# A cross-attention and FFN kernel: work handed between engines is taken up a slot later, with four projection banks and one bank for p times V

## The reference

```python
h = _layernorm(x)                                # x: 32 batches x 64 rows x 512
q = (h @ Wq)                                     # 32 heads of 128, Wq 512 x 4096
k, v = ctx @ Wk, ctx @ Wv                        # 8 heads of 128 each
q, k = rope(q), rope(k)                          # tables gathered by position
scores = where(mask == 0, -1e9, q k^T / sqrt(128))   # four q heads share one k and v head
x = x + (softmax(scores) @ v) @ Wo
packed, scales = quantize_to_mxfp4(kernel)       # 512 x 512, blocks of 32 rows
x = x + _layernorm(x) @ dequantize(packed, scales) + bias
```

## Time and profile before

| what | value |
| --- | --- |
| median of 3 runs | 1244.49 us (1240.0 to 1246.65) |
| the profiled execution | 1243.1 us |
| its span, first to last instruction | 1240.9 us |
| PE busy | 1157.4 us, 93% |
| DVE busy | 1032.9 us, 83% |
| ACT busy | 653.5 us, 53% |
| POOL busy | 503.4 us, 41% |
| DMA | 67.41 MB, mean 54 GB/s |

### The profile page before, as it was taken

How to read it: one execution, slowest core, us unless ns; L and a number is a source line. 1 busy time by engine, 2 the same in 40 slices (tenths; PEclk the granted TensorE clock), 3 DMA queues, 4 the chain that set the end, 5 groups by cost and what they waited for, 6 DMA issues and landing times.

```text
span 1240.9 us, 19680 instructions
## 1 busy us (share of the span) xinstructions
PE 1157.4 (93%) x6308; PEld 983.0 (79%) x6320; DVE 1032.9 (83%) x2003; ACT 653.5 (53%) x2169; POOL 503.4 (41%) x394
## 2 busy tenths in 40 slices
PE   3799989999999999997988999999999999999987
PEld 2578878887888878886777788888888888888864
DVE  5878999899989999878888887787777877777786
ACT  3255545555555555645453545555555655555561
POOL 5353443335342443445543434433353434342322
PEclk7999999999999999998998999999999999999999
DMA  5220111112111021112312223111021112110003
GB/s 171 77 77 23 52 43 43 48 31 60 39 41 42 27 68 40 51 45 89 108 54 74 77 86 93 45 35 35 26 60 36 43 27 60 30 48 18 26 26 102
DMA packets 41476, 67.41 MB, mean 54 GB/s; under 512 B 8992, under 2 KB 11168, under 8 KB 41376
## 3 DMA queue, kind: packets, MB, share of 16 engines
q1 hardware_dynamic: 40608, 64.05, 17.6%
q0 software_dynamic: 768, 2.10, 0.5%
HBM read 61.94 MB, written 4.19 MB: 53 GB/s over the span
## 4 chain that ended last, share of the span: by engine, by line
PE 66%; DVE 19%; ACT 4%; issue 4%; DMA 4%; POOL 2%; SPq 0%; ACTq 0%; DVEq 0%; POOLq 0%
PE proj L379 11%; PE proj L380 11%; PE proj L381 10%; PE pO L379 6%; PE pS L468 6%; PE pO L380 6%; PE pO L381 6%; DVE t L728 2%; DVE t L729 2%; PE pV L495 2%; DMA raw<-wo 2%; PE pV L496 2%; PE pT L478 2%; ACT sm L641 2%; PE pO L512 1%
## 5 line engine op out<-in xcount | busy, mean ns | idle before, releaser
L952 POOL TENSOR_TENSOR qT<-qT,t 128x512 f32<-128x512 f32 x128 | 187.3, 1463 | 393.3 <-DVE t L729 393.2
L619 ACT ACTIVATE sm<-pS 128x256 f32<-128x256 f32 x128 | 49.3, 385 | 313.7 <-PE pS L468 313.5
L641 ACT ACTIVATE sm<-sm,tiny 128x64 f32<-128x64 f32 x512 | 172.0, 337 | 77.0 <-DVE tiny L847 75.2
L379 PE MATMUL proj<-XH,QH 128*128 128x512 f32 x512 | 204.8, 400 | 6.1 <-DVE VS L899 4.1
L380 PE MATMUL proj<-XL,QH 128*128 128x512 f32 x512 | 202.6, 396 | 0.0
L381 PE MATMUL proj<-XH,QL 128*128 128x512 f32 x512 | 202.6, 396 | 0.0
L379 PE MATMUL pO<-OH,AH 128*128 128x512 f32 x448 | 181.1, 404 | 12.1 <-DVE acc L815 12.0
L380 PE MATMUL pO<-OL,AH 128*128 128x512 f32 x448 | 176.6, 394 | 0.0
L381 PE MATMUL pO<-OH,AL 128*128 128x512 f32 x448 | 175.9, 393 | 0.0
L468 PEld LDWEIGHTS pS<-kT,qT 128*128 128x128 f32 x1024 | 134.7, 192 | 13.2 <-issue 3.1
L724 DVE TENSOR_TENSOR qT<-proj,COS 128x512 f32<-128x512 f32 x128 | 88.0, 687 | 68.0 <-PE proj L381 40.2
(11 more groups left out here) (129 smaller groups left out, 2565.2 us busy)
## 6 DMA issues: line engine op xcount, KB each, us to landing
raw<-wq SPq DMA_DIRECT2D x64, 256.0 KB
raw<-wo SPq DMA_DIRECT2D x64, 256.0 KB
acc<-x SPq DMA_DIRECT2D x16, 256.0 KB, 3.0
raw<-wk SPq DMA_DIRECT2D x16, 256.0 KB
raw<-ctxT SPq DMA_DIRECT2D x16, 256.0 KB
raw<-wv SPq DMA_DIRECT2D x16, 256.0 KB
rawm<-fbias SPq DMA_DIRECT2D x16, 256.0 KB, 2.8
out<-acc SPq DMA_DIRECT2D x16, 256.0 KB, 2.0
```

Of the source, the lines that this page charges most:

```text
L379: pe.matmul(dst, lh, rh, start=k == 0, stop=False)
L641: made = act.activation(v4[:, a], v4[:, a], ACT.Exp, bias=nmx[:, a:a + 1], accum_out=rsum[:, a:a + 1])
L952: pool.tensor_tensor(dst, dst, t2[:, :].rearrange("p (a t) -> p a t", t=64), ALU.add).then_inc(made, 1)
```

## The change

The order inside ACT's, DVE's and POOL's slots is new, `proj` has four banks instead of three, and the two halves of `pV` lie in one bank. No arithmetic instruction and no DMA is added or removed. PE's order stays, except that the transposes of the second half's rows come a slot earlier (`X_AT` starts at HALF - 5 instead of HALF - 4).

- ACT: the high parts of V, x, the FFN input and W4 are taken up in the slot after the one in which PE made them (n - 1), at the start of the slot, and `high(n, False)` follows them, ahead of the scores. AH moves behind the exponentials.
- DVE: V's low part, `x_low` and `f_low` are those of slot n - 1 and stand, with the streamed low parts and `quantise`, between the statistics and the rotation of q. The reciprocal and the product come before AL.
- POOL: `low(n, False)` comes before the rotation's addition.

```diff
-PROJ = 3
+PROJ = 4
-X_AT = {-2: 4, -1: 5, 0: 6, 1: 7} | {HALF - 4 + t: 8 + t for t in range(8)}
+X_AT = {-2: 4, -1: 5, 0: 6, 1: 7} | {HALF - 5 + t: 8 + t for t in range(8)}
-        pV = pb("pV", [128, 2, 512])
+        pV = pb("pV", [128, 2, 256])
@@ PE, scores
+                if m == 0:
+                    pe.wait_ge(a_cs, 16)
@@ ACT, slot n
                 high(n, True)
+                if v_tile(n - 1):
+                    v_high(n - 1)
+                for i, c in quant_parts(n - 1):
...
+                if n - 1 in X_AT:
+                    x_high(X_AT[n - 1])
+                if n - 1 in FFN_AT and not is_last(n - 1):
+                    f_high(FFN_AT[n - 1])
+                high(n, False)
                 if 0 <= m < PAIRS:
                     act.wait_ge(e_qk, m + 1)
...
-                if 0 <= m - 2 < PAIRS:
-                    act.wait_ge(e_pv, m - 1)
...
                     made.then_inc(a_ex, 1)
+                if 0 <= m - 2 < PAIRS:
+                    act.wait_ge(e_pv, m - 1)
...
@@ DVE, slot n
+                if v_tile(n - 1):
...
+                if n - 1 in X_AT:
+                    x_low(X_AT[n - 1])
+                if n - 1 in FFN_AT and not is_last(n - 1):
+                    f_low(FFN_AT[n - 1])
+                for i in streamed(n, False):
+                    if lo_on_dve(i):
...
+                for i, c in quant_parts(n):
+                    for step in PART[c] if c < 14 else ():
+                        quantise(i, step).then_inc(v_q, 1)
                 if 0 <= n < PAIRS:
                     s, h = n // 4, n % 4
                     dve.wait_ge(e_qp, n + 1)
...
-                if 0 <= m - 2 < PAIRS:
-                    dve.wait_ge(a_ah, m - 1)
...
                 if 0 <= m < PAIRS:
...
                     dve.tensor_tensor(v4, v4, rinv.unsqueeze(2).broadcast_to([128, 4, 64]), ALU.mult).then_inc(v_pn, 1)
+                if 0 <= m - 2 < PAIRS:
+                    dve.wait_ge(a_ah, m - 1)
...
@@ POOL, slot n
                 low(n, True)
+                low(n, False)
                 if 0 <= n < PAIRS:
                     add_turned(qT[:, n // 4 % 2, :, n % 4, :], v_qc, v_qs, n + 1, g_qr)
                 if n in FFN_AT and not is_last(n):
                     add_bias(FFN_AT[n])
-                low(n, False)
```

More of the change, by code:

```diff
@@ L257, in cs_turned @@
         def cs_turned(T):
-            where = (pS, pT, pO, pV[:, 0])[T] if T < 4 else pS
+            where = (pS, pT, pO, pV.rearrange("p b t -> p (b t)"))[T] if T < 4 else pS
             return where[:, 256:512].rearrange("p (k t) -> p k t", k=2)
@@ L604, in rope, with v_high @@
                 act.copy(SIN[:, c], cs_turned(T)[:, 1, :]).then_inc(a_cs, 1)
+            def v_high(n):
+                s, t = v_tile(n)
+                v = v_count(s, t)
+                b = BANK["v", v - 1]
+                act.wait_ge(e_vp, v)
+                if s >= 2:
+                    act.wait_ge(e_pv, 4 * (s - 2) + t + 1)
+                for i in range(2):
+                    act.copy(VS[ROWS[i], i, 4 * (s % 2) + t, :], proj[ROWS[i], b, 0:256]).then_inc(a_vh, 1)
             for T in range(4):
@@ L643, in _ @@
                     made.then_inc(a_ex, 1)
+                if 0 <= m - 2 < PAIRS:
+                    act.wait_ge(e_pv, m - 1)
+                    if m - 2 >= 2:
+                        act.wait_ge(e_op, m - 3)
+                    act.copy(AH[:, m % 2].rearrange("p h (b t) -> p b h t", b=2),
+                             pV[:, :, :].rearrange("p b (h t) -> p b h t", h=4)).then_inc(a_ah, 1)
                 if is_last(n):
                     f_high(FFN_AT[n])
-                high(n, False)
                 if n in ROPE_AT:
                     rope(ROPE_AT[n])
[L649 to L667, removed]
         @block.vector
@@ L819, in _ @@
                     statistics("f", FFN_AT[n])
+                if v_tile(n - 1):
+                    s, t = v_tile(n - 1)
+                    v = v_count(s, t)
+                    b = BANK["v", v - 1]
+                    dve.wait_ge(a_vh, 2 * v)
+                    for i in range(2):
+                        made = dve.tensor_tensor(VS[ROWS[1 - i], i, 4 * (s % 2) + t, :], proj[ROWS[i], b, 0:256],
+                                                 VS[ROWS[i], i, 4 * (s % 2) + t, :].bitcast(F32), ALU.subtract)
+                    made.then_inc(v_vl, 1)
+                if n - 1 in X_AT:
[4 more added lines that the diff above has]
+                    if lo_on_dve(i):
+                        _, kind, a, b = STREAM[i]
+                        hi, lo, _, view = weight(kind, a, b)
+                        dve.wait_ge(a_hi, i + 1)
+                        dve.tensor_tensor(lo, view(raw[:, i % RING, :]), hi.bitcast(F32),
+                                          ALU.subtract).then_inc(v_lo, 1)
+                for i, c in quant_parts(n):
+                    for step in PART[c] if c < 14 else ():
+                        quantise(i, step).then_inc(v_q, 1)
                 if 0 <= n < PAIRS:
@@ L869, in _ @@
                     dve.tensor_tensor(v4, v4, rinv.unsqueeze(2).broadcast_to([128, 4, 64]), ALU.mult).then_inc(v_pn, 1)
[L870 to L880, removed]
+                if 0 <= m - 2 < PAIRS:
+                    dve.wait_ge(a_ah, m - 1)
+                    dve.tensor_tensor(AL[:, m % 2].rearrange("p h (b t) -> p b h t", b=2),
+                                      pV[:, :, :].rearrange("p b (h t) -> p b h t", h=4),
+                                      AH[:, m % 2].rearrange("p h (b t) -> p b h t", b=2).bitcast(F32),
+                                      ALU.subtract).then_inc(v_al, 1)
                 k = mask_at(n)
@@ L892, in _ @@
                            (g_qr, n + 1))
[L893 to L910, removed]
         @block.gpsimd
```

21 lines of the change are left out of this document (11 added, 10 removed).

## The result

The changed kernel takes 1275.4 us (median of 4 runs, 1274.1 to 1276.0), the kernel before 1243.1 beside it (4 runs): a ratio of 1.026, with a 95% interval of 1.023 to 1.029. It is 2.6% slower. The forecast of 1245 was wrong, and the time lies above the range's end of 1262.

A forecast was written before the change was run, and what follows sets the result against it. It took DVE to bound slots 16 to 56 and PE the second half. Terms +8.4 + 3.0 - 3.5 - 3.5 - 2.0 - 1.5 = +0.9 gave 1244.0, with 1.4 for the median 1245; range 1225 to 1262.

The forecast's parts named there:

- Slots 8 to 56: Per slot +0.70 for exponentials, -0.375 for listed waits, -0.15 for collisions: +0.175, or +8.4 us over 48 slots.
- the two credits: Slots 8 to 56: listed waits fall into the new one, at most -0.375 a slot; shorter POOL collisions, -0.15 of 0.35.
- the exposed exponentials: Slots 8 to 56: with AL moved behind, DVE stands for ACT's exponentials before the reciprocal, +0.70 us a slot.
- VectorE is full, not late: Slots 16 to 56: DVE is the bound, occupied or about to issue for 340 of 355 us.
- Slots 61 to 69: Forecast for slots 60 to 68: ACT's third-piece wait stands before sm and holds PE, +3 us, ends -4 and +9.
- Four banks and the FFN stage: FFN slots: V's bank wait goes, -2.2, and its slow clock, -1.3; k's stays. Sum -3.5 us, between 0 and -8.
- Start: Start: POOL frees a q piece's low part earlier, taking -3.5 of ACT's 4.17 us wait, ends 0 and -6.
- Second half and tail: PE's idle time in the second half goes, -1.5 us; the tail's wait for exponentials goes in part, -2 us.
- C: Rival: exposed exponentials and blocked ACT, with no collision relief and X at +9: +14.1 us, 1259; chance 0.23.
- A: Rival: DVE is late, not full; slots 16 to 56 run at PE's pace, -16 us: 1218, half 1231; chance 0.18.
- B: Rival: DVE's collisions with POOL go entirely, 9.6 us less than the sum: 1236; chance 0.12.
- the signs that I named: Slots 16 to 56: reciprocal's wait some 25 us, V's low part unwaited, quantising means nearer 0.55 us, 362 us in all.

The follow-up runs named there:

- Experiment 1: The changed kernel with AH and AL back in their old places: 1241.2 us; the kernel before with only AH and AL moved: 1268.7 us.
- experiment 5: Quantise steps moved: in the changed kernel between PL and reciprocal, 1249.4 us; in Experiment 4's first kernel behind AL, 1234.1, or behind the product, 1232.4.
- experiment 2: The kernel before with four projection banks and pV in one bank, no order changed: 1240.7 us, ratio 0.999.
- Experiment 4: The changed kernel with AH and AL back and ACT's and POOL's weight splits late in X's 8 slots: 1231.5 us; with X also a slot later: 1240.9.
- Experiment 6: Experiment 4's first kernel with ACT's high part of V ahead of the first pieces of weights: 1228.5 us, ratio 0.990.
- first kernel of experiment 5: The changed kernel with the quantise steps between PL and the reciprocal: 1249.4 us, ratio 1.007 to the kernel before.

## Why the prediction was wrong, point by point

**Slots 8 to 56: +8.4 forecast, +20.4 measured.** This is the step that failed: the two credits set against the exposed exponentials. The parts, for the 40 slots from 16 to 56, where the forecast comes to +7.0 and the measurement, in equal windows, is +21.5:

```text
us, 40 slots                       forecast   measured
wait for the exponentials            28.0       28.9
other listed waits                    0          8.1
  (against 15.0 and 15.7 before)    +13.0      +21.3
VectorE's busy time (collisions)     -6.0       -0.5
between instructions                  0         +0.7
sum                                  +7.0      +21.5
```

The term for the exposed exponentials, 0.70 us a slot, was right: 0.72 in every slot. Two credits against it were not. First, I let all 15.0 us of the listed waits fall into the new one, which is the most that they could give. 8.1 came back, and 7.1 of it is a wait that the kernel before did not list in these slots: quantising, put at the front of the slot, reached its two loads before they had landed (4.2 and 2.9 us). I had asked what each moved step waits for on other engines, and not on the DMA queue.

Second, I took 6 us of relief from the collisions, on the ground that the overlap would get shorter. The busy time fell by 0.5 us. At 328 us quantising, the rotation's addition and the early low part run side by side; that this is so throughout I did not show. The prediction had named this very case, 0.51 us a slot with neither relief nor more than half of the waits, and the measurement, 21.5 / 40 = 0.54, lies just above that. Experiment 1 points the same way from the other side: the moves without the softmax's order gave 1.5 us, where the two credits came to 0.525 x 40 = 21. Part of the first credit was to come from the new wait taking others in, and this kernel can't show that part. Taking one credit in full and near half of the other was the error: the cost was read from rows, the credits were guessed.

The reading of the kernel before was slightly off as well. Its 355.0 us for the 40 slots are 357.4 in an equal window, so PE lost some 18 us to its own pace and not 16. That changes no term.

The Trainium skill (SBUF — State Buffer, "Who interferes with whom") says that the port pair that VectorE and GpSimd share is held by one of them at a time. The traces agree: a step took 426 ns in experiment 5, away from POOL's operations, and two of them took 2.47 us beside two operations of POOL in the changed kernel.

**VectorE is full, not late.** Right for the kernel before and after, shown by experiments 1 and 2: a wait of 0.7 us a slot comes out in the time nearly one for one. But full isn't the whole of it. In experiment 5 VectorE's busy time fell by some 15 us and the slots took 491. There VectorE waits for TensorE (18.7 us in the first of its kernels) and TensorE for VectorE (7.9 us) in turn, which looks as if the chain of one pair around both engines held the slot up. No run took that chain apart, so this is argued and not shown, and how far below 490 a different order could go stays open.

**Slots 61 to 69: +3 forecast, +8.4 measured.** The mechanism was the one named, and the upper end of +9 was near. The size was off, since the first piece's load (4.12 us) is waited for as well, and since slots 62 and 64 both lose. One sign that I had named for being wrong came with it: ACT's blocks cost PE over 10 us, 6.16 and 7.98 in these two slots alone. Experiment 4 shows the mechanism: split late again, the 8 slots take 89.4 us.

**Four banks and the FFN stage: -3.5 forecast, -1.5 measured.** The banks alone give 6.6 (experiment 2), with V's wait gone. The prediction's -1.3 for the slow clock is given without a working; with the banks alone TensorE's busy time fell by 3.6. In the changed kernel V's wait stood again, 2.46 us, since V's high part had been moved behind pieces of weights whose load is late. Experiment 6 shows that. k's bank wait stayed, as forecast.

**Start: -3.5 forecast, -3.8 measured at slot 5, -0.7 at slot 8.** The mechanism came: at 46.74 ACT splits the piece of the earlier trace rows without a wait. The agreement of the numbers is in part luck. The kernel with the banks alone reaches slot 5 1.8 us earlier too, with no order changed, and in the changed kernel slots 5 to 8 give back 3.2 us of the 3.8. TensorE waits 2.7 us there for the softmax's product, and 0.7 before. The prediction has no term for that.

**Second half and tail: -1.5 and -2 forecast, +2.2 and +2.9 measured.** The 32 slots from 93 to 125 gained 1.1, as TensorE has hardly any idle time there. Slot 78 took 10.8 us in place of 7.0: `acc` stood behind a reciprocal that waited 0.72 us and behind k's rotation, and TensorE waited 1.88 us for it, half of the loss. The other half is the clock behind that wait. The nine matmuls that follow start about 0.43 us apart, and those after them 0.23. The granted clock of these 3.73 us is 0.54, near the lower of its two levels (1.2 GHz):

```profile
789.37:793.10 3.73, 3.73 (x10) 2.94 (x10) 3.52 (x6) 0.00 (x0) 3.73 (x4) 0.54 0.25 59
```

With the softmax's order back slots 77 to 93 take 135.2 us, and with it alone in the kernel before 135.6. So this loss needs that order and the other moves together.

In the tail I said that the wait for the exponentials would go in part. It grew, from 0.77 in the earlier trace rows to 1.71 in the worst of the slots without q:

```profile
1211.95 0.18 DVE L893 RECIPROCAL tiny<-tiny 128x4 f32<-128x4 f32 x1 [1.29 <-ACT sm L662]
...
1217.25 0.18 DVE L893 RECIPROCAL tiny<-tiny 128x4 f32<-128x4 f32 x1 [1.71 <-ACT sm L662]
```

I had counted that `AH` no longer stands ahead of the exponentials, and had forgotten that `AL` no longer covers them: the same 0.7 us that I charged elsewhere. Experiment 1 takes 2.1 of the tail's 2.9 back.

**The rivals.** C was the mechanism that came. Its 1259 lacks the waits that did not fall away (some 8 to 10 us over 48 slots), the smaller gains in the start and the FFN, and the losses in slots 77 to 93 and in the tail. A and B did not come: the 40 slots did not get shorter, and the busy time fell by 0.5 us, of 14. Of the signs that I named, the wait of the reciprocal (28.9 for some 25) and k's bank wait came as said. V's low part waits for almost nothing (1.0 for 7.9). The quantising means of 0.62 to 0.70 and the 378.9 us for 362 did not.

## What to carry to other kernels

Before a step is moved out of the gap between a request to another engine and its answer, ask what else fills the gap on that engine: on a full engine the open gap costs its whole length in every round, here 0.72 us times 40. Work that is ready at any time can stand in the gap. A step that waits for a load holds up whatever stands behind it: in the stage of X that was worth 9 us, while for quantise's loads in slots 5 to 61 moving it away gained nothing. A step handed over later must keep its place against late loads in the receiving queue, and the steps of one chain on two queues move together or not at all (ACT's high part moved alone cost another 81 us). Price what a reordering takes from rows, and its credits by their lower bound unless a row shows them too.

## What the runs showed of the hardware that I had not expected

- The eight slots of X, with TensorE's waits of 6.16 and 7.98 us in them, ran at a granted clock of 0.88, where before it was 0.93. In slot 78 a wait of 1.88 us was followed by 3.73 us at 0.54. In slots 16 to 56, with 20.5 us without a matmul in place of 12.8, it fell from 1.00 to 0.97, and the same matmuls were busy 13.8 us longer, with no listed wait of VectorE for them.
- Small steps of VectorE changed their length with their place too: L765, on 128 x 8 numbers, took a mean of 322 ns in the changed kernel, where the same step took 172 in the kernel before, and L781 took 344 for 515. In the first kernel of experiment 5 both took 172.
- The collisions of VectorE with POOL, some 15 us of busy time in 40 slots, could be taken away without any gain in time (experiment 5).
